# A fourth PSUM place for gathered rows in round two of a graph network kernel

## The reference

```python
w = relu(edgefeats @ fnet_w1 + fnet_b1) @ fnet_w2 + fnet_b2
W = w.reshape(-1, 16, 16)
for _ in range(2):
    xj = hx[edge_src]
    m = einsum('ei,eio->eo', xj, W)
    agg = segment_sum(m, edge_dst, 12500) * inv_deg[:, None]
    hx = gru_cell(agg, hx, ...)
return layernorm(x + hx)
```

## Time and profile before

| | us |
|---|---|
| time, median of 3 runs | 5143.58 (5143.08 to 5144.82) |
| profiled execution, first to last instruction | 6694.6 |
| PE busy in it | 5648.0 |
| DVE busy | 4296.9 |
| POOL busy | 3811.1 |
| ACT busy | 3179.0 |

### The profile page before, as it was taken

One profiled execution on the slowest core, in us unless ns is written; L12 is line 12 of the kernel. 1 busy time (PEld: TensorE's weight loads), 2 busy tenths in 40 slices (PEclk: granted clock), 3 DMA queues, 4 the chain that ended last, 5 costly groups with the idle time before them and its releaser, 6 DMA issues.

```text
span 6694.6 us, 119595 instructions
## 1 busy us (share of the span) xinstructions
PE 5648.0 (84%) x38360; PEld 4666.6 (70%) x38361; DVE 4296.9 (64%) x7146; ACT 3179.0 (47%) x5259; POOL 3811.1 (57%) x4021
## 2 busy tenths in 40 slices
PE   2888888888888888888858888888888888888887
PEld 1777777777777777777647777776777777777775
DVE  3766666666666666666636666666666666666665
ACT  1554555445554545454325454454545454444442
POOL 6355555555555555555555555555555555555553
PEclk7988998889898999998878898898988889888887
DMA  4111111111111111111111111111111111111110
GB/s 107 46 34 48 34 48 34 48 34 48 34 48 44 39 48 34 48 34 48 25 47 29 40 29 40 33 37 39 31 40 29 40 29 41 29 40 29 40 29 20
DMA packets 197656, 263.32 MB, mean 39 GB/s; under 512 B 95745, under 2 KB 165942, under 8 KB 184205
## 3 DMA queue, kind: packets, MB, share of 16 engines
q1 hardware_dynamic: 61885, 216.66, 9.5%
q0 software_dynamic: 128192, 33.07, 4.8%
q10 hardware_dynamic: 7026, 6.21, 0.4%
HBM read 195.73 MB, written 54.92 MB: 37 GB/s over the span
## 4 chain that ended last, share of the span: by engine, by line
PE 65%; issue 14%; another core or an unknown queue 10%; ACT 6%; DVE 3%; DVEq 1%; DMA 0%; POOL 0%; ACTq 0%; POOLq 0%; SPq 0%
PE ps_all L722 45%; PE ps_all L732 8%; ACT src_hot L603 3%; PE ps_all L755 3%; PE ps_all L745 3%; PE ps_all L709 3%; PE ps_all L776 2%; ACT src_hot L607 2%; DVE shared L1137 1%; DVE fan L1092 1%; PE ps_all L762 0%; ACT shared L576 0%; ACT h_sb L570 0%; DVE xg L1145 0%
## 5 line engine op out<-in xcount | busy, mean ns | idle before, releaser
L722 PE MATMUL ps_all<-parts,src_hot 125*128 125x400 f32 x18048 | 3820.4, 368 | 258.7 <-issue 166.4
L722 PEld LDWEIGHTS ps_all<-parts,src_hot 125*128 125x128 f32 x18048 | 3501.9, 202 | 482.6 <-issue 367.7
L535 POOL DMA_INDIRECT xg<-in_x,idx x2027 | 1923.4, 949 | 1394.3 <-issue 556.1
L535 POOL DMA_INDIRECT xg<-h_rows,idx x1979 | 1873.1, 946 | 1371.6 <-issue 518.7
L1137 DVE TENSOR_TENSOR shared<-ps_all,at_hot 128x400 f32<-128x400 f32 x2256 | 1211.8, 566 | 1858.8 <-remote 1168.4
L603 ACT ACTIVATE src_hot<-keys,neg_key 128x384 fp32r<-128x384 int16 (+1 forms) x3072 | 1617.0, 599 | 1653.1 <-remote 979.0
L732 PE MATMUL ps_all<-fan,h_sb 128*32 128x160 f32 x12544 | 825.0, 316 | 489.5 <-issue 435.8
L1092 DVE TENSOR_TENSOR fan<-xg,ps_all 128x1280 f32<-128x1280 f32 x784 | 1158.8, 1478 | 88.0 <-DVE xg L1145 33.4
L607 ACT ACTIVATE src_hot<-src_hot 128x1536 fp32r<-128x1536 f32 (+1 forms) x768 | 1122.2, 1461 | 72.3 <-ACT src_hot L603 2.8
L1145 DVE TENSOR_REDUCE xg<-shared 128x48 f32<-128x1200 f32 (+1 forms) x768 | 1056.7, 1376 | 75.6 <-DVE shared L1137 1.0
L732 PEld LDWEIGHTS ps_all<-fan,h_sb 128*32 128x32 f32 x12544 | 391.8, 111 | 842.4 <-issue 794.9
(11 more groups left out here) (120 smaller groups left out, 1383.7 us busy)
## 6 DMA issues: line engine op xcount, KB each, us to landing
keys<-key_d SPq DMA_DIRECT2D x96, 768.0 KB
h_d<-h_sb SPq DMA_DIRECT2D x49, 1056.0 KB
h_sb<-h_d SPq DMA_DIRECT2D x49, 1056.0 KB
xg<-in_x,idx POOLq DMA_INDIRECT x2027
xg<-h_rows,idx POOLq DMA_INDIRECT x1979
ef<-in_ef_t SPq DMA_DIRECT2D x49, 420.0 KB
acc_all<-agg_t SPq DMA_DIRECT2D x1, 3161.0 KB
idx<-in_src_tiles SPq DMA_DIRECT2D x98, 32.0 KB
```

Of the source, the lines that this page charges most:

```text
L535: pool.indirect_dma_start(out=xg[:, buf, at, 0:C], out_offset=None, in_=rows_of, in_offset=bass.IndirectOffsetOnAxis(ap=idx[:, buf, at:at ...
L722: last = pe.matmul(ps_g[j], src_hot[0:KP, k % 2, kb, j * P:(j + 1) * P], parts[0:KP, m, kb, :], start=(kb == 0 and m == 0), stop=(kb == KB ...
```

## The change

In round two, halves 2 and 6 of a super get a fourth tile from PE; round one stays. So POOL fetches 38 tiles of a super in round two where it fetched 40, and PE makes 26 where it made 24. The fourth place for the product is bank 2. The buffers of the one-hots of even halves grow to four tiles, those of odd halves stay at three (two tensors in place of one). The key rows (`keys`, one DMA per super, both rounds) and `at_hot` grow from 24 tiles to 26. To make room, `prod_x` and `hot_x` move into `shared`, `picked` begins at 3920 and has four slots, `at_pe` becomes int16, and `whole_row` and `whole_col` of the set-up lie elsewhere. `slot_free` looks back as many halves as it must, since slot 3 is used only every fourth half.

```diff
-BY_PE = ((2, 3, 3, 3, 3, 3, 3, 3), (3, 3, 3, 3, 3, 3, 3, 3))
+BY_PE = ((2, 3, 3, 3, 3, 3, 3, 3), (3, 3, 4, 3, 3, 3, 4, 3))
 GT = [max(r[k] for r in BY_PE) for k in range(HPS)]
 TG = sum(GT)
+SOURCES = [max(GT[k] for k in range(m, HPS, 2)) for m in range(2)]
+SLOTS = max(GT)
+PICKED = 3920
...
-        back = 1 if BY_PE[rnd][k - 1] > j else 2
+        back = [b for b in range(1, HPS + 1) if BY_PE[rnd][k - b] > j][0]
...
-        shared = sb("shared", [P, 4320 + 3 * C * AR])
+        shared = sb("shared", [P, PICKED + SLOTS * C * AR])
...
-        prod_x = sb("prod_x", [P, C, C])
+        prod_x = shared[:, 2560:2560 + C * C].rearrange("p (o i) -> p o i", o=C)
...
-        at_pe = sb("at_pe", [P, NSUP * TG])
+        at_pe = sb("at_pe", [P, NSUP * TG], I16)
-        src_hot = sb("src_hot", [P, 2, KB, max(GT) * P], F32R)
+        src_hot = [sb(f"src_hot{m}", [P, KB, SOURCES[m] * P], F32R) for m in range(2)]
...
-        ps_g = [ps_all[:, b * BANK:b * BANK + AR * C] for b in (3, 6, 5)]
+        ps_g = [ps_all[:, b * BANK:b * BANK + AR * C] for b in (3, 6, 5, 2)]
...
-                                pick_rows(rnd, s + 1, k - 1, (2,))
+                                pick_rows(rnd, s + 1, k - 1, (2, 3))
```

More of the change, by code:

```diff
@@ L174, in gnn_program @@
         own = shared[0:GROUP, 3640:3640 + 2 * CA * TQ]
-        near_tmp, far_tmp = (shared[:, lo:lo + CHUNK * TPB] for lo in (3920, 4120))
-        picked = shared[:, 4320:4320 + 3 * C * AR].rearrange("p (m c a) -> p m c a", m=3, a=AR)
+        near_tmp, far_tmp = (shared[:, lo:lo + CHUNK * TPB] for lo in (PICKED + 3 * C * AR, PICKED + 3 * C * AR + CHUNK * TPB))
+        picked = shared[:, PICKED:PICKED + SLOTS * C * AR].rearrange("p (m c a) -> p m c a", m=SLOTS, a=AR)
         agg_sb = sb("agg_sb", [P, TPB * WIN])
@@ L190, in gnn_program @@
         h_xt = sb("h_xt", [HA, P])
-        prod_x = sb("prod_x", [P, C, C])
+        prod_x = shared[:, 2560:2560 + C * C].rearrange("p (o i) -> p o i", o=C)
         msg_x = sb("msg_x", [P, CNT + 1])
-        hot_x = sb("hot_x", [P, XWIN])
+        hot_x = shared[:, 2560 + C * C:2560 + C * C + XWIN]
         keys = sb("keys", [P, 2, TG * P], I16)
-        at_pe = sb("at_pe", [P, NSUP * TG])
+        at_pe = sb("at_pe", [P, NSUP * TG], I16)
         parts = sb("parts", [P, PARTS, KB, AR * C], F32R)
-        src_hot = sb("src_hot", [P, 2, KB, max(GT) * P], F32R)
+        src_hot = [sb(f"src_hot{m}", [P, KB, SOURCES[m] * P], F32R) for m in range(2)]
         neg_key = sb("neg_key", [P, KB])
@@ L224, in gnn_program @@
         nodes_part = [parts[0:KP, m].rearrange("p k w -> p (k w)") for m in range(PARTS)]
-        key_row, whole_row, src_col, key_col = (
+        key_row, src_col, key_col = (
             acc_all[0:p, (TPR + m) * P:(TPR + m) * P + w] for p, m, w in
-            ((2 * NSUP, 20, TG * P // 2), (2 * NSUP, 32, TG * P // 2), (P, 44, NSUP * TG), (P, 54, NSUP * TG)))
-        whole_col = at_pe[:]
+            ((2 * NSUP, 20, TG * P // 2), (P, 36, NSUP * TG), (P, 48, NSUP * TG)))
+        whole_row = fan[:].rearrange("p k a b c -> p (k a b c)")[0:2 * NSUP, 0:TG * P // 2]
+        whole_col = acc_all[:, (TPR + 20) * P:(TPR + 20) * P + NSUP * TG]
         key_out = src_row.bitcast(I16)[:, 0:TG * P // 2]
@@ L602, in src_hots @@
                 for kb in range(KB):
-                    act.activation(src_hot[:, k % 2, kb, 0:some * P], keys[:, buf, first * P:(first + some) * P],
+                    act.activation(src_hot[k % 2][:, kb, 0:some * P], keys[:, buf, first * P:(first + some) * P],
                                    ACT.Abs, bias=neg_key[:, kb:kb + 1]).then_inc(s_src_far, 1)
                 act.wait_ge(s_src_far, KB * (HPS * (rnd * (NSUP - 1) + s - 1) + k + 1))
-                hot_of = src_hot[:, k % 2, :, 0:some * P]
+                hot_of = src_hot[k % 2][:, :, 0:some * P]
                 act.activation(hot_of, hot_of.bitcast(F32), ACT.Relu, bias=1.0, scale=-1.0).then_inc(s_src_hot, some)
@@ L721, in gather_rows @@
                         for m in range(PARTS):
-                            last = pe.matmul(ps_g[j], src_hot[0:KP, k % 2, kb, j * P:(j + 1) * P], parts[0:KP, m, kb, :],
+                            last = pe.matmul(ps_g[j], src_hot[k % 2][0:KP, kb, j * P:(j + 1) * P], parts[0:KP, m, kb, :],
                                              start=(kb == 0 and m == 0), stop=(kb == KB - 1 and m == PARTS - 1))
@@ L1196, in emit @@
                             if not is_last(i):
-                                pick_rows(rnd, s + 1, k - 1, (2,))
+                                pick_rows(rnd, s + 1, k - 1, (2, 3))
                                 keep_rows(rnd, s + 1, 1 - buf, k - 1)
                         elif not is_first(i, par):
-                            pick_rows(rnd, s, HPS - 1, (2,))
+                            pick_rows(rnd, s, HPS - 1, (2, 3))
                             keep_rows(rnd, s, buf, HPS - 1)
```

## The result

The kernel after takes 5188.19 us (5187.66 to 5190.91), the kernel before 5144.2 in the same comparison: ratio 1.0085, 95% interval 1.0073 to 1.0097. That is 44 us slower, where 56 were forecast.

The account below looks back on a forecast made before the run. POOL was taken to bound round two at 50.0 us per super, PE at 48.3; two tiles bring PE to 51.2, +1.2 over 47 supers, +56 on 5143.6: 5200 us, own range 5175 to 5265, 8 in 10 5085 to 5285.

Parts of the forecast that it names:

- Which engine bounds which kernel: Round two: POOL at 50.0 us per super before, PE 1.7 behind; PE at 51.2 after; chance 0.50.
- the distance of POOL's DMAs, 1.25 us: POOL starts one indirect DMA every 1.25 us, so 40 in a super of round two take 50.0 us.
- that sum: Whole time of the kernel before if POOL never waits: 5151.5 us, 8 us above the median.
- 69.4 us between the rounds: Time from POOL's last DMA start of round one to its first of round two, a term of the whole-time sum.
- 74.3 at the end: Time that follows POOL's last DMA start, a term of the whole-time sum, in us.
- The price of a tile on PE: Each added tile in round two costs PE 1.47 us, two 2.94 per super, with nothing to hide them.
- Rival (a): PE's record is inflated even where clean, so POOL leads by more and the change pays: 5092 or 5026 us; chance 0.27.
- half 0 ... 8.44 us: PE's half 0 in round two, recorded at 9.69 us, takes 8.44 without its two gaps in the aggregate.
- 39.85 + 2.94 = 42.79: PE's halves 1 to 7 of a round-two super plus the two added tiles, in us.
- The end behind the last super changes by nothing: The time behind the last super was taken as unchanged, adding nothing to the forecast.
- DVE and ACT as cover: Per super of round two, DVE rises to 45.6 us and ACT to 34.6, below PE's 51.2; late one-hot taken as 0.
- the bursts: Slow issue of PE's weight loads, 1.1 to 1.3 us apart, two or three per super, read as recording or program-fetching cost.

Follow-up runs that it names:

- two_left_out: Kernel before with two of POOL's DMAs left out per super of round two but its first, made by nobody: 5057.17 us, ratio 0.983.
- pe_once: Kernel before with the third tile's eight matmuls done twice in half 2 of round two, POOL still at 40 DMAs: 5146.73 us, ratio 1.0003.
- half_priced: Kernel after with each fourth tile multiplied by the node table's upper part alone, four matmuls in place of eight: 5122.46 us, 0.9956 of the kernel before.
- first and third group: Two of three groups of four experiment kernels, each group on its own chip; every run in these two took 6500 to 6790 us.
- before_2: The kernel before, unchanged, run again in the third group for a profile: 6683.7 us beside 6706.6 for its comparison runs.
- odd_halves: Kernel after with the two fourth tiles in halves 3 and 7 in place of 2 and 6: 6506.86 us, 0.9694 of the kernel before.

## Why the prediction was right, and where it was not

**Which engine bounds which kernel: right, and shown.** POOL before (two_left_out, pe_once), PE after (its trace, and half_priced). The one row that carried this was the distance of POOL's DMAs, 1.25 us, counted over the whole kernel. Two terms of that sum came from the stretched trace: 69.4 us between the rounds and 74.3 at the end. In pe_once, with the same 40 DMAs, they are 62.9 and 69.6, and the sum would have been 5140 in place of 5151.5, 4 us under the time in place of 8 over it.

**The price of a tile on PE: right.** 1.47 us was forecast, 1.44 to 1.46 stand in the trace after. Rival (a) is refuted: the clean halves of a stretched trace are those of an undisturbed execution, to 0.02 us in halves 1, 3 and 5. The matmul pitch is the same too, 4.30 us for 24 loads, and eight loads more take 1.46, 0.18 us each. What the Trainium skill's page "TensorE: Matmul & The Clock Gate" gives in its section "Wait — 56ns, not 53.3ns?" is an estimated 169 ns for such a matmul, and the trace does not agree with it where each of them has weights of its own to load.

**The sum: three terms mis-sized, partly against each other.** The step "half 0 ... 8.44 us" took two gaps out of 9.69 and left the rest. It measured 8.17, 13 us less over 47 supers. The other halves sum to 42.76 after the change, against 39.85 + 2.94 = 42.79 in the prediction, so an undisturbed super took 50.93 in place of 51.2. The two starts of PE's loop stood in the sum at nothing; they gave back 10 us, and the mean super after is 51.14, nearly the forecast. "The end behind the last super changes by nothing" failed too, as far as pe_once can stand for the kernel before: from the first products of super 48 to the end it takes 96.7 us (5048.89 to 5145.6) and the kernel after 87.1 (5099.66 to 5186.8). In pe_once POOL is still issuing its last DMAs for 27 us of that, in the kernel after for 19. Between the traces of these two, supers 1 to 47 differ by 49.6 us, the end by -9.6 and the part ahead by 1.2, together the 41 us between their spans. That 0.93 x 47 is 44, the measured loss, is therefore chance in part: it leaves out the loop's starts and the end, which cancel.

**DVE and ACT as cover: right.** 1957 / 43.2 = 45.3 us of DVE per super (45.6 forecast) and 1447 / 43.2 = 33.5 of ACT (34.6). PE was idle 5 us in 2200, all of it for DVE's spread, so no one-hot was late.

**What the bursts are: wrong.** "I read them as the cost of recording, or of fetching the program while it is recorded" is refuted in its first half by the timed runs of the first and third group; that fetching the program takes part is neither shown nor excluded. The reading of the earlier trace rows was off as well: the sixteen loads don't come singly 1.1 to 1.3 us apart, ten come at their usual distance and the rest in groups of one to three behind gaps of that length. The forecast still held, because taking the bursts out gave the other kind of execution, the kind that the timed runs of the comparison were. The known time of 5143.6 us said that its own runs had no room for the bursts; that the comparison's runs would be of the same kind was luck, since the prediction didn't know of two kinds. Had they been stretched, the forecast would in all likelihood have failed on the sign: on such executions 25 tiles were 1.3 to 1.7% faster than 24, and 26 tiles, in other halves, 3.1%. The kernel after itself wasn't run there. What makes an execution stretched, and why more gather shortens its bursts, stays open.

**Where the optimum lies.** With POOL at 50.0 - 1.25 n and PE at 48.0 + 1.46 n for n more tiles, they cross at n = 0.7. One tile gives 49.5 us per super, 25 us less over the round; half_priced, with the same PE work but one DMA fewer on POOL, showed 22 of them. A complete 25-tile kernel was measured on stretched executions alone, 1.7% faster; near 5.1 ms its gain is argued, not shown.

## What to carry to other kernels

When work moves from one engine to another, write both engines' time per period, before and after, and look for the crossing: here the receiver had 1.9 us of room and was given 2.9. When a profiled execution is much longer than the time, don't scale its shares; take the undisturbed periods at full clock, count the instructions of fixed distance through the whole kernel, and see whether the sum meets the time. Look at the places where a loop starts over and at the end as well: here they were worth 10 us each, nearly the whole miss of 12. Adding an engine's work alone, and taking away the other's alone, settles who bounds in two runs.

## What was not expected of the hardware

The same program runs in 5.14 ms or in 6.7 ms, with all runs of a group of one kind, and each group on one chip (10 and 5 for the long kind, 9 for the short). Whether the kind belongs to the chip is not shown, since no chip was used for two groups. The long kind has bursts in which PE's loads stop again and again for 0.5 to 1.3 us while nothing holds them: gaps over 0.5 us take 11.7 us of a super in before_2, 6.9 in odd_halves and 0.1 in the kernel after. The granted clock then drops to its lower level, 615 of the 2700 us in before_2 and 338 in odd_halves. In that kind the sign of this change's core is turned round. Two tiles more on PE shortened a super there (round two's 65.2 us in before_2 to 61.6 in odd_halves, each from the first products of its super 1 to those of super 47, divided by 46), although they are 2.9 us of work more.
